# Cross-attention kernel: query weights on SyncE's queue, x in two parts around the first mask, one norm of twelve tiles behind eight maxima, and the shift placed ahead of two loads

## The chip, the cores and the metric

The kernel runs on one core of a Trainium2 chip. TensorE (PE in the rows, PEld for its weight loads), VectorE (DVE), ScalarE (ACT), GpSimd (POOL) and SyncE (SP) each work through their own instructions in order and meet at semaphores. DMAs are issued from the queues of SyncE (SPq) and ScalarE (ACTq). The metric is the time of one execution in device microseconds, as the median of several runs; a profiled execution gives the trace.

## The reference

Cross-attention with 16 heads of 8 over 32 batches, then a feed-forward block with quantised weights and activations. What is computed:

```
x   [32, 56, 128]   ctx [32, 1500, 128]   mask [32, 1, 56, 1500]
q = heads(layernorm(x) @ Wq + bq);  k = heads(ctx @ Wk + bk);  v = heads(ctx @ Wv + bv)
scores = where(mask == 0, -1e9, q k^T / sqrt(8))
x = x + (softmax(scores) v) @ Wo + bo
h = gelu(quant(layernorm(x)) @ ternary(w1)^T)
x = x + quant(h) @ ternary(w2)^T
```

## The kernel before

The work goes batch by batch, and every engine's order is written out by hand in tables of tokens (`PE_PASS`, `ACT_PASS`, `DVE_PASS`, `POOL_PASS`), one row of tokens per step. A step works on several batches at once: it takes the exponentials of batch b while it finds the maxima of batch b+1 and makes the keys of batch b+2. So two steps stand ahead of the first one that has all of it: `open` makes the keys of batch 0, and `lead` finds the maxima of batch 0 and makes the keys of batch 1. Then come `first_even`, `first_odd`, a loop of fourteen pairs of steps, two last steps and a tail.

The tokens that matter here. On TensorE: `T0` to `T2` turn a third of a batch's context (4 transposes each, L841), `K0` to `K2` make a third of the keys (L844), `V0` to `V2` of the values (L848), `X0` to `X3` turn four normalised tiles of x (L856), `Q0` to `Q7` project them (L858, two instructions of one `Q` to a row in a list of instructions), `F0` spreads a flag (L851), `M0` to `M11` are two matmuls each for the maxima (L902), `R0` turns the maxima (L853). On ScalarE `T`, `X` and `V` copy out of PSUM (L697, L702, L707), `sum` adds up a mask (L687), `kf` and `kh` make the keys and their rounded part (L717, L727). On VectorE `norm` normalises tiles of x (L1010 to L1043), `Q` takes a projection (L1143), `some` and `F0` make the flagged queries `q_flag` (L1120 to L1134), `bias` turns a mask into a bias (L1113), `m0` to `m23` take the maxima (L1206), two for each `M`. GpSimd makes the low part of the keys, `k_lo` (`kl`, L621 and L624), and the rounded and masked queries (`q`, L604 to L609), in the order `kl0 q0 kl1 kl2`.

PSUM has seven banks that go round in the order of TensorE's tokens; a token waits until what was in its bank has been taken. TensorE's `T0` of a step also waits until that batch's context has landed, and `M0`, `M4` and `M8` until a third of the keys has been placed.

SyncE places the keys (`place_keys`: for each third, wait for `k_lo`, two DMAs, wait for a copy, two more DMAs), places the shift (`place_shift`: wait for `shift_ready`, which VectorE sets after `R0`, then two DMAs that the first score matmul waits for, L930), and loads contexts and masks (`load`: 750 KB of context, then 656 KB of mask in two DMAs). It does these in one order, so each wait holds back all that stands behind it.

Of the kernel before, what the change touches and what calls it, by code (L numbers as in the profile page):

```python
# [205 lines left out]
def xattn_ffn(nc, x, ctx_in, mask, wq, bq, wk, bk, wv, bv, wo, bo, w1, w2, out):  # L206
    es = ExitStack()
    with es:
# [215 lines left out]
        def _(sp):  # L424
# [4 lines left out]

            def load(bt):  # L430
                b, k, p = bt
                at_ctx, at_mask = b * (SK * D), b * (SQ * SK)
                turned, biased = NSEG * (b - 1), NSEG * (b - 1)
                if not isinstance(b, int):
                    at_ctx, at_mask = sp.snap(at_ctx), sp.snap(at_mask)
                    turned = biased = sp.snap(turned)
                wait(sp, ctx_t_ready, turned)
                src = ctx_flat[bass.ds(at_ctx, SK * D)].rearrange("(c k d) -> k c d", k=KC, d=D)
                sp.dma_start(ctx_sb[:, p], src).then_inc(ctx_loaded[p], 16)
                wait(sp, mask_biased, biased)  # L440
                load_mask(at_mask, p)
# [222 lines left out]
        def _(act):  # L664

            ctx_0 = ctx_flat[0:SK * D].rearrange("(c k d) -> k c d", k=KC, d=D)
# [3 lines left out]
            act.dma_start(wk_sb[:], wk).then_inc(wk_loaded, 16)  # L670
            act.dma_start(bk_sb[:], bk.rearrange("(p a) -> p a", a=1)).then_inc(wk_loaded, 16)
            wq_groups = wq.rearrange("k (h g r) -> k g h r", h=2, g=2)
            bq_groups = bq.rearrange("(h g r a) -> h g r a", h=2, g=2, a=1)
            for g in range(2):
                for a in range(2):
                    act.dma_start(wq_sb[:, g, :].rearrange("k (h a r) -> k h a r", h=2, a=2)[:, :, a, :],
                                 wq_groups[:, g]).then_inc(wq_loaded, 16)
                    for h in range(2):
                        at = SLOT * h + GR * a
                        act.dma_start(bq_sb[at:at + GR, g:g + 1], bq_groups[h, g]).then_inc(wq_loaded, 16)  # L680
# [616 lines left out]
```

## Time and profile before

| | us |
|---|---|
| median of 3 runs | 914.86 |
| lowest and highest | 913.99, 914.88 |
| the profiled execution | 913.98 |
| its span in the trace | 912.3 |

The trace is of the profiled execution, so what is read from it is set against 913.98 us, of which 1.7 us lie outside the span; the median is 0.88 us above it. Times in the trace count from the start of the span. A row of the timeline gives the start, the time taken by the merged instructions, the engine, the line and operation, the tiles and shapes, the count, and in brackets how long the engine had been idle and what ended that. [...]

### The profile page before, as it was taken

How to read it: one execution, taken by the hardware profiler on the slowest of the kernel's cores; microseconds unless marked ns; L12 is line 12 of the kernel's file. 1: busy time of each engine (PE TensorE's matmuls, PEld its weight loads, DVE VectorE, ACT ScalarE, POOL GpSimd, SP SyncE). 2: the span in 40 equal slices, each digit the busy share in tenths (PEclk: the TensorE clock that was granted, in tenths of full speed). 3: DMA queues.
4: the chain of work that ended last, by engine and by line, in shares of the span. 5: the costliest groups of instructions: out<-in, count | busy, mean ns of one | idle time of the engine just before them, and what ended most of it. 6: DMA issues, size and time to landing. Idle time of an engine off the chain costs nothing.

```text
span 912.3 us, 33988 instructions
## 1 busy us (share of the span) xinstructions
PE 841.9 (92%) x11724; PEld 634.5 (70%) x11724; DVE 766.7 (84%) x2599; ACT 701.5 (77%) x1272; POOL 303.7 (33%) x360
## 2 busy tenths in 40 slices
PE   1676989999999999999999999999999999999993
PEld 1335767777777777777777777777777777777772
DVE  4887679888898989888898989888898989888954
ACT  1345768978797888979797888979797888979671
POOL 5512352323433333323433333322433333323300
PEclk9888999999999999999999999999999999999996
DMA  5433223343233333343233333343233323340100
GB/s 134 107 78 87 53 65 94 91 101 90 65 92 81 92 82 97 88 106 86 65 90 80 93 80 97 88 107 86 65 91 80 93 80 97 88 108 23 37 2 6
DMA packets 79000, 74.01 MB, mean 81 GB/s; under 512 B 10250, under 2 KB 75258, under 8 KB 78970
## 3 DMA queue, kind: packets, MB, share of 16 engines
q1 hardware_dynamic: 75695, 72.65, 31.0%
q10 hardware_dynamic: 3275, 0.97, 0.5%
q8 instruction: 18, 0.29, 0.1%
q14 instruction: 12, 0.10, 0.0%
HBM read 47.97 MB, written 0.92 MB: 54 GB/s over the span
## 4 chain that ended last, share of the span: by engine, by line
PE 64%; DVE 18%; issue 10%; ACT 3%; ACTq 2%; DMA 1%; DVEq 1%; SPq 1%; POOL 0%; POOLq 0%
PE ps_p L917 10%; PE ps_v L964 10%; PE ps_p L902 10%; PE ps_p L923 6%; PE ps_p L930 6%; PE ps_p L848 6%; PE ps_p L844 6%; DVE spare L1206 4%; PE ps_p L841 4%; DVE mask_bias L1113 1%; DVE row_stat L1025 1%; DVE row_stat L1026 1%; DVE row_stat L1024 1%; PE ps_p L872 1%; PE ps_p L868 1%
## 5 line engine op out<-in xcount | busy, mean ns | idle before, releaser
L1206 DVE CUSTOM_DVE_ANT_0 spare<-ps_p,mask_bias 120x500 bf16<-120x500 f32 x744 | 467.3, 673 | 49.0 <-PE ps_p L902 38.3
L737 ACT ACTIVATE probs<-ps_p 125x448 f32<-125x448 f32 x768 | 352.5, 559 | 57.1 <-PE ps_p L930 53.1
L621 POOL TENSOR_TENSOR k_lo<-k_full,keys 128x500 fp32r<-128x500 f32 x96 | 127.5, 1328 | 255.6 <-ACT keys L727 238.8
L917 PE MATMUL ps_p<-qry_lo,keys 64*125 64x448 f32 x768 | 162.8, 418 | 7.7 <-DVE seg_max L1206 2.6
L902 PE MATMUL ps_p<-keys,qry_hi 64*120 64x500 f32 x768 | 157.5, 430 | 5.6 <-DVE seg_max L1206 5.4
L964 PE MATMUL ps_v<-probs,vals 125*32 125x112 f32 x6144 | 160.7, 260 | 0.3 <-ACT probs L737 0.3
L964 PEld LDWEIGHTS ps_v<-probs,vals 125*32 125x32 f32 x6144 | 145.2, 110 | 22.4 <-issue 22.1
L923 PEld LDWEIGHTS ps_p<-qry_hi,keys 64*125 64x125 f32 x1536 | 146.0, 184 | 8.5
L930 PE MATMUL ps_p<-own_query,mask_bias 57*125 57x448 f32 x768 | 144.8, 370 | 7.5 <-DMA own_query<-shift 7.5
L923 PE MATMUL ps_p<-qry_hi,keys 64*125 64x224 f32 x1536 | 145.6, 266 | 0.0
L917 PEld LDWEIGHTS ps_p<-qry_lo,keys 64*125 64x125 f32 x768 | 72.5, 182 | 64.9 <-DVE seg_max L1206 33.0
L717 ACT ACTIVATE k_full<-ps_p,bk_sb 128x500 f32<-128x500 f32 x96 | 65.0, 677 | 65.7 <-PE ps_p L844 61.1
L604 POOL TENSOR_TENSOR q_hi<-q_flag,ones_f 128x112 fp32r<-128x112 f32 x32 | 13.7, 427 | 284.4 <-DVE q_flag L1134 284.4
L902 PEld LDWEIGHTS ps_p<-keys,qry_hi 64*120 64x120 f32 x768 | 69.2, 179 | 51.9 <-issue 20.8
L848 PE MATMUL ps_p<-wv_sb,ctx_t 128*125 128x128 f32 x768 | 102.8, 278 | 1.0 <-DVE seg_max L1206 1.0
L844 PE MATMUL ps_p<-ctx_t,wk_sb 128*128 128x500 f32 x192 | 101.8, 614 | 1.2 <-DVE seg_max L1206 1.1
L727 ACT ACTIVATE keys<-k_full 128x1000 fp32r<-128x1000 f32 x96 | 97.8, 1037 | 0.7
L848 PEld LDWEIGHTS ps_p<-wv_sb,ctx_t 128*125 128x125 f32 x768 | 92.0, 189 | 2.7 <-issue 1.6
L930 PEld LDWEIGHTS ps_p<-own_query,mask_bias 57*125 57x125 f32 x768 | 74.2, 186 | 8.0 <-DMA own_query<-shift 8.0
L697 ACT ACTIVATE ctx_t<-ps_p 128x500 f32<-128x500 f32 x96 | 55.0, 591 | 31.7 <-PE ps_p L841 31.7
L841 PE MATMUL ps_p<-ident,ctx_sb 125*128 125x125 f32 x384 | 59.0, 285 | 14.3 <-DMA ctx_sb<-in_ctx_dram 10.7
L841 PEld LDWEIGHTS ps_p<-ident,ctx_sb 125*128 125x128 f32 x384 | 46.7, 148 | 36.2 <-issue 20.1
(127 smaller groups left out, 885.1 us busy)
## 6 DMA issues: line engine op xcount, KB each, us to landing
keys<-k_lo SPq DMA_DIRECT2D x384, 62.5 KB, 2.0
ctx_sb<-in_ctx_dram SPq DMA_DIRECT2D x31, 750.0 KB
mask_sb<-in_mask_Bx1xSxS_ik_dram SPq DMA_DIRECT2D x64, 328.1 KB
own_query<-shift SPq DMA_DIRECT2D x64, 1.8 KB
out_dram<-x_rows SPq DMA_DIRECT2D x16, 56.0 KB, 1.6
ctx_sb<-in_ctx_dram ACTq DMA_DIRECT2D x3, 250.0 KB
x_rows<-in_x_dram SPq DMA_DIRECT2D x1, 672.0 KB, 12.7
w_sb<-in_L_ffn_w_dram SPq DMA_DIRECT2D x2, 256.0 KB, 7.2
```

The lines of the kernel that those rows point to most:

```text
L621: pool.tensor_tensor(k_lo[:, (p + n) % 2, :], k_full[:, (p + n) % 2, :], keys[:, p, 0, at].bitcast(F32), ALU.subtract)\
L727: act.activation(keys[:, p, 0:2, at], k_full[:, (p + n) % 2, :].rearrange("p (g k) -> p g k", g=1).to_broadcast([D, 2, SEG]), ACT.Copy).th ...
L737: act.activation(probs[:, (c + NG * p) % NP, h], ps_p[0:KC, BANK[how]["S", c, h], 0:HC], ACT.Exp)\
L841: mm = pe.transpose(bank[:, c * KC:(c + 1) * KC], ctx_sb[:, p, 4 * n + c, :], ident[0:KC, 0:KC])
L844: mm = pe.matmul(bank[:, 0:SEG], wk_sb[:], ctx_t[:, p, n * SEG:(n + 1) * SEG], start=True, stop=True)
L848: mm = pe.matmul(bank[0:KC, c * D:(c + 1) * D], ctx_t[:, p, at:at + KC], wv_sb[:], start=True, stop=True)
L902: pe.matmul(ps_p[0:MROWS, BANK[how]["M", n, h], 0:SEG], qry_hi[rows, p, 2 * r:2 * r + 2, :].rearrange("p a q -> p (a q)")[:, 0:MROWS], key ...
L917: pe.matmul(score_bank(c, h, how), keys[rows, p, 0, at], qry_lo[rows, p, :, :], start=True, stop=False, skip_group_check=True)
L923: pe.matmul(score_bank(c, h, how)[:, heads, :], keys[rows, p, 1 + g, at], qry_hi[rows, p, heads, 0:SQ], start=False, stop=False, skip_grou ...
L930: mm = pe.matmul(score_bank(c, h, how), mask_bias[rows, p, c * KC:(c + 1) * KC], own_query[rows, p, :, :], start=False, stop=True, skip_gr ...
L964: mm = pe.matmul(ps_v[r:r + VT, col:col + PAIR], with_ones(p, c, t), src, start=(c == 0 and t < 4), stop=(c == NC - 1), skip_group_check=True)
L1206: dve.tensor_tensor_reduce(junk, ps_p[0:MROWS, BANK[how][slot], 0:SEG], mask_bias[0:MROWS, p, s * SEG:(s + 1) * SEG].bitcast(F32), 1.0, LO ...
```

## The change

Six edits, all of them around the two steps ahead of the first full one.

- The query weights and biases go from ScalarE's queue (12 DMAs behind the context of batch 0) to SyncE's queue (8 DMAs, right behind the first four tiles of x). On ScalarE's queue the key weights now stand ahead of the context. ScalarE runs one small activation before its first wait.
- The other twelve tiles of x are sent when the first mask has landed, no longer right behind it.
- `norm` of these twelve tiles is one chain over all twelve, where there were three chains of four; it stands in `lead` behind `m7`. `X1` to `X3` and `Q2` to `Q7` all stand in `lead` behind it. The normalised tiles have a place of their own (in `probs`).
- On SyncE the keys of batch 0 are placed ahead of the load of batch 1's context and mask; they stood behind it.
- Batch 2's context is loaded ahead of batch 1's keys, and its mask behind the placing of the first shift, with `w1`, `w2` and the rows of `wo` behind that. They stood ahead of batch 1's keys.
- TensorE's wait for the rows of `wo` is at `W` in `first_odd`, no longer ahead of `first_even`.

```diff
 PE_PASS = passes(
-    "T0 X0 T1 T2 Q0 Q1 K0 F0 K1 K2 X1 Q2 Q3",
-    "M0 M1 T0 M2 T1 X2 M3 T2 Q4 Q5 M4 K0 M5 M6 K1 M7 X3 M8 K2 Q6 Q7 M9 V0 M10 F0 V1 M11 V2 R0",
+    "T0 X0 T1 T2 Q0 Q1 K0 K1 F0 K2",
+    "M0 M1 M2 T0 M3 T1 T2 K0 M4 K1 X1 Q2 Q3 M5 K2 M6 X2 Q4 Q5 V0 M7 X3 M8 Q6 Q7 V1 M9 F0 V2 M10 M11 R0",
...
 ACT_PASS = passes(
-    "T0 X0 T1 T2 sum kf0 kh0 kf1 kh1 kf2 kh2 X1",
-    "T0 T1 X2 T2 sum kf0 kh0 kf1 kh1 X3 kf2 kh2 V0 V1 V2",
+    "T0 X0 T1 T2 sum kf0 kh0 kf1 kh1 kf2 kh2",
+    "T0 T1 T2 sum kf0 kh0 kf1 kh1 X1 kf2 kh2 X2 V0 X3 V1 V2",
...
 DVE_PASS = passes(
-    "norm1 Q0 Q1 some F0 bias0 norm2 bias1 bias2 Q2 Q3",
-    "m0 m1 norm3 m2 m3 m4 m5 Q4 Q5 m6 m7 m8 m9 m10 m11 m12 m13 some m14 m15 Q6 Q7 "
-    + " ".join(f"m{n}" for n in range(16, 20)) + " F0 m20 m21 m22 m23 neg R0 bias0 bias1 bias2",
+    "Q0 Q1 some F0 bias0 bias1 bias2",
+    "m0 m1 m2 m3 m4 m5 m6 m7 norm1 m8 m9 Q2 Q3 m10 m11 m12 m13 Q4 Q5 some m14 m15 m16 m17 Q6 Q7 "
+    + " ".join(f"m{n}" for n in range(18, 20)) + " F0 m20 m21 m22 m23 neg R0 bias0 bias1 bias2",
...
             sp.wait_ge(mask_edge[0], 2)
             load_mask(0, 0)
+            sp.wait_ge(mask_loaded[0], 32)
             sp.dma_start(x_rows[:, 4:NT], x_groups[:, 4:NT]).then_inc(x_loaded[1], 16)
-            sp.wait_ge(ctx_loaded[0], 16)
-            sp.wait_ge(mask_edge[1], 2)
-            load(batch(0, 1))
-            sp.dma_start(wv_sb[:], wv).then_inc(wv_loaded, 16)
-            sp.dma_start(w1_sb[:], w1.rearrange("(a p) i -> p a i", p=128)).then_inc(ff_loaded, 16)
-            sp.dma_start(w2_sb[:], w2).then_inc(ff_loaded, 16)
-
             for n in range(NSEG):
                 place_keys(batch(0, 0), n)
+            load_context(batch(0, 1))
+            sp.wait_ge(mask_edge[1], 2)
+            load_mask_of(batch(0, 1))
+            sp.dma_start(wv_sb[:], wv).then_inc(wv_loaded, 16)
...
-            load(batch(0, 2))
+            load_context(batch(0, 2))
+            for n in range(NSEG):
+                place_keys(batch(0, 1), n)
+            place_shift(batch(0, 0))
+            load_mask_of(batch(0, 2))
+            sp.dma_start(w1_sb[:], w1.rearrange("(a p) i -> p a i", p=128)).then_inc(ff_loaded, 16)
+            sp.dma_start(w2_sb[:], w2).then_inc(ff_loaded, 16)
             sp.wait_ge(halves_known, 1)
...
-            for n in range(NSEG):
-                place_keys(batch(0, 1), n)
-            place_shift(batch(0, 0))
             step(batch(0, 0))
...
+            act.wait_ge(consts, 1)
+            act.activation(warm[:], ones_f[0:1, 0:1], ACT.Copy)
             act.wait_ge(wk_loaded, 32)
...
-                dve.wait_ge(x_loaded[min(g, 1)], 16)
-                if g > 1:
-                    dve.wait_ge(xn_copied, g - 1)
-                statistics(chain(group_step, 20 * g), x_rows[:, 4 * g:4 * g + 4, :], xn_stat[:], 4)
...
+                first, tiles = (0, 4) if g == 0 else (4, NT - 4)
+                dve.wait_ge(x_loaded[g], 16)
+                st = xn_stat[:, :, first:first + tiles]
+                statistics(chain(group_step, 20 * g), x_rows[:, first:first + tiles, :], st, tiles)
```

On SyncE's queue, from the first load to the placing of batch 1's keys, before (the first 1x8x56 row, `own_query`, is the shift; x_rows of 12 tiles are the rest of x):

```order
L506 DMA x_rows<-in_x_dram 112x4x128
L428 DMA mask_sb<-in_mask_Bx1xSxS_ik_dram 56x1500 x2
L509 DMA x_rows<-in_x_dram 112x12x128
L439 DMA ctx_sb<-in_ctx_dram 125x12x128
L428 DMA mask_sb<-in_mask_Bx1xSxS_ik_dram 56x1500 x2
L513 DMA wv_sb<-in_L_xattn_Wv_dram 128x128
L514 DMA w_sb<-in_L_ffn_w_dram 128x4x128
L515 DMA w_sb<-in_L_ffn_w_dram 128x512
L464 DMA keys<-k_lo 32x500 x12
```

And the same queue in the changed kernel, from the rest of x to the weights behind the shift:

```order
L529 DMA x_rows<-in_x_dram 112x12x128
L474 DMA keys<-k_lo 32x500 x12
L439 DMA ctx_sb<-in_ctx_dram 125x12x128
L430 DMA mask_sb<-in_mask_Bx1xSxS_ik_dram 56x1500 x2
L535 DMA wv_sb<-in_L_xattn_Wv_dram 128x128
L536 DMA wo_sb<-in_L_xattn_Wo_dram 128x128
L537 DMA bv_sb<-in_L_xattn_bv_dram 128x1
L538 DMA bo_sb<-in_L_xattn_bo_dram 112x128
L439 DMA ctx_sb<-in_ctx_dram 125x12x128
L474 DMA keys<-k_lo 32x500 x12
L459 DMA own_query<-shift 1x8x56 x2
L430 DMA mask_sb<-in_mask_Bx1xSxS_ik_dram 56x1500 x2
```

Batch 1's context, the fourth load of SyncE before, now stands behind the twelve DMAs that place batch 0's keys, and each third of those waits for GpSimd's `k_lo`.

On TensorE, from the projections of the first four tiles to the turning of batch 1's context, before (`qry_hi` and `keys` are the maxima's matmuls, `ident,ctx_sb` the turning of a third of a context, `ident,spare` that of four tiles of x):

```order
L858 MATMUL ps_p<-spare,wq_sb 128x448 x2
L844 MATMUL ps_p<-ctx_t,wk_sb 128x500
L851 MATMUL ps_p<-some_diag,ones_bf 128x56
L844 MATMUL ps_p<-ctx_t,wk_sb 128x500 x2
L856 MATMUL ps_p<-ident,spare 128x112 x4
L858 MATMUL ps_p<-spare,wq_sb 128x448 x2
L902 MATMUL ps_p<-keys,qry_hi 120x500 x4
L841 MATMUL ps_p<-ident,ctx_sb 128x125 x4
L902 MATMUL ps_p<-keys,qry_hi 120x500 x2
```

And from the same projections in the changed kernel, as far as the second four tiles of x:

```order
L872 MATMUL ps_p<-spare,wq_sb 128x448 x2
L858 MATMUL ps_p<-ctx_t,wk_sb 128x500 x2
L865 MATMUL ps_p<-some_diag,ones_bf 128x56
L858 MATMUL ps_p<-ctx_t,wk_sb 128x500
L916 MATMUL ps_p<-keys,qry_hi 120x500 x6
L855 MATMUL ps_p<-ident,ctx_sb 128x125 x4
L916 MATMUL ps_p<-keys,qry_hi 120x500 x2
L855 MATMUL ps_p<-ident,ctx_sb 128x125 x8
L858 MATMUL ps_p<-ctx_t,wk_sb 128x500
L916 MATMUL ps_p<-keys,qry_hi 120x500 x2
L858 MATMUL ps_p<-ctx_t,wk_sb 128x500
L870 MATMUL ps_p<-ident,probs 128x112 x4
```

`X1`, `Q2` and `Q3` have left the stretch ahead of the maxima; the turning of batch 1's context comes after `M2` where it came after `M1`, and `M3` to `M11` still stand behind it.

## Rows read from the trace of the kernel before

**Rows 1.** The page, part 1: busy time, share of the span and instructions:

```profile
PE 841.9 (92%) x11724; PEld 634.5 (70%) x11724; DVE 766.7 (84%) x2599; ACT 701.5 (77%) x1272; POOL 303.7 (33%) x360
```

**Rows 2.** Windows, a stretch of `lead`: busy us by engine, PEclk, DMA share, GB/s:

```profile
41.10:54.80 13.70, 8.51 (x26) 4.84 (x26) 10.21 (x42) 3.73 (x6) 2.89 (x6) 0.51 0.47 114
```

**Rows 3.** Timeline of TensorE in the opening and at the first score matmul:

```profile
13.40 1.04 PE L841 MATMUL ps_p<-ident,ctx_sb 125*128 125x125 f32 x4
18.29 1.10 PE L841 MATMUL ps_p<-ident,ctx_sb 125*128 125x125 f32 x4 [3.85 <-DMA ctx_sb<-in_ctx_dram]
24.01 3.33 PE L858 MATMUL ps_p<-spare,wq_sb 128*128 128x448 f32 x4 [4.63 <-DMA bq_sb<-in_L_xattn_bq_dram]
...
30.40 3.47 PE L844 MATMUL ps_p<-ctx_t,wk_sb 128*128 128x500 f32 x4
...
43.19 0.77 PE L902 MATMUL ps_p<-keys,qry_hi 64*120 64x500 f32 x2
...
78.78 0.74 PE L930 MATMUL ps_p<-own_query,mask_bias 57*125 57x448 f32 x2 [6.49 <-DMA own_query<-shift]
```

**Rows 4.** Timeline of VectorE, from the wait for the query biases to the flagged queries:

```profile
23.90 0.88 DVE L1010 BATCH_NORM_STATS2 xn_stat<-x_rows 112x6 f32<-112x128 f32 x4 [9.75 <-DMA bq_sb<-in_L_xattn_bq_dram]
...
42.55 0.67 DVE L1206 CUSTOM_DVE_ANT_0 probs<-ps_p,mask_bias 120x500 bf16<-120x500 f32 x1
...
43.74 0.87 DVE L1010 BATCH_NORM_STATS2 xn_stat<-x_rows 112x6 f32<-112x128 f32 x4
44.65 0.39 DVE L1014 BATCH_NORM_AGGREGATE xn_stat<-xn_stat 112x2 f32<-112x6 f32 x4
...
47.46 1.12 DVE L1043 TENSOR_SCALAR spare<-x_rows,xn_stat 112x128 f32<-112x128 f32 x4
48.49 0.67 DVE L1206 CUSTOM_DVE_ANT_0 probs<-ps_p,mask_bias 120x500 bf16<-120x500 f32 x1
...
53.16 0.68 DVE L1143 TENSOR_SCALAR q_all<-ps_p,bq_sb 128x448 f32<-128x448 f32 x1 [2.19 <-PE ps_p L858]
...
66.13 0.27 DVE L1134 TENSOR_TENSOR q_flag<-q_all,ps_p 128x112 f32<-128x112 f32 x1
```

**Rows 5.** Timeline of ScalarE: the table, the first keys, the sum of the weights:

```profile
19.62 1.28 ACT L697 ACT_TABLE_LOAD   x1 [19.62 <-issue]
...
28.21 0.68 ACT L717 ACTIVATE k_full<-ps_p,bk_sb 128x500 f32<-128x500 f32 x1 [3.91 <-PE ps_p L844]
...
86.04 0.63 ACT L742 ACTIVATE wtern<-w_sb 128x512 f32<-128x512 f32 x1
```

**Rows 6.** Timeline of GpSimd: the masked queries of batch 0:

```profile
33.05 1.15 POOL L607 TENSOR_TENSOR qry_hi<-head_of_row,q_hi 128x448 fp32r<-128x448 f32 x1
```

**Rows 7.** Timeline of SyncE's queue: what is issued, merged by kind:

```profile
4.20 0.78 SPq L428 DMA_DIRECT2D mask_sb<-in_mask_Bx1xSxS_ik_dram  x2
...
31.38 10.34 SPq L464 DMA_DIRECT2D keys<-k_lo  x12
...
76.24 1.47 SPq L449 DMA_DIRECT2D own_query<-shift  x2
77.75 0.46 SPq L439 DMA_DIRECT2D ctx_sb<-in_ctx_dram  x1
78.26 6.31 SPq L428 DMA_DIRECT2D mask_sb<-in_mask_Bx1xSxS_ik_dram  x2
91.81 2.46 SPq L464 DMA_DIRECT2D keys<-k_lo  x4
```

**Rows 8.** Windows while one context is loaded alone, columns as in rows 2:

```profile
77.70:79.00 1.30, 0.22 (x2) 0.22 (x4) 0.00 (x0) 0.00 (x0) 0.00 (x0) 0.50 0.02 5
79.00:81.00 2.00, 2.00 (x14) 1.83 (x16) 0.00 (x0) 1.25 (x3) 0.00 (x0) 0.50 0.27 82
81.00:84.50 3.50, 3.41 (x32) 2.59 (x30) 2.19 (x7) 3.10 (x8) 0.00 (x0) 0.88 0.36 109
84.50:87.00 2.50, 2.50 (x18) 1.33 (x16) 2.50 (x9) 2.28 (x7) 0.00 (x0) 1.00 0.88 212
```

More of the change, by code:

```diff
@@ L428, in load_mask, with load_context, load_mask_of @@
                     sp.dma_start(mask_sb[at:at + SQ, p, :], src).then_inc(mask_loaded[p], 16)
-            def load(bt):
[L431 to L441, printed above, removed]
+            def load_context(bt):
+                b, k, p = bt
+                at, turned = b * (SK * D), NSEG * (b - 1)
+                if not isinstance(b, int):
+                    at, turned = sp.snap(at), sp.snap(turned)
+                wait(sp, ctx_t_ready, turned)
+                src = ctx_flat[bass.ds(at, SK * D)].rearrange("(c k d) -> k c d", k=KC, d=D)
+                sp.dma_start(ctx_sb[:, p], src).then_inc(ctx_loaded[p], 16)
+            def load_mask_of(bt):
+                b, k, p = bt
+                at, biased = b * (SQ * SK), NSEG * (b - 1)
+                if not isinstance(b, int):
+                    at, biased = sp.snap(at), sp.snap(biased)
+                wait(sp, mask_biased, biased)
+                load_mask(at, p)
+            def load(bt):
+                load_context(bt)
+                load_mask_of(bt)
             def place_shift(bt):
@@ L506, in _ @@
             sp.dma_start(x_rows[:, 0:4], x_groups[:, 0:4]).then_inc(x_loaded[0], 16)
+            wq_groups = wq.rearrange("k (h g r) -> k g h r", h=2, g=2)
+            bq_groups = bq.rearrange("(h g r) -> h r g", h=2, g=2)
+            for a in range(2):
+                for g in range(2):
+                    sp.dma_start(wq_sb[:, g, :].rearrange("k (h a r) -> k h a r", h=2, a=2)[:, :, a, :],
+                                 wq_groups[:, g]).then_inc(wq_loaded, 16)
+                for h in range(2):
+                    at = SLOT * h + GR * a
+                    sp.dma_start(bq_sb[at:at + GR, :], bq_groups[h], allow_slow_non_contiguous=True).then_inc(wq_loaded, 16)
             sp.wait_ge(mask_edge[0], 2)
             load_mask(0, 0)
+            sp.wait_ge(mask_loaded[0], 32)
             sp.dma_start(x_rows[:, 4:NT], x_groups[:, 4:NT]).then_inc(x_loaded[1], 16)
-            sp.wait_ge(ctx_loaded[0], 16)
-            sp.wait_ge(mask_edge[1], 2)
-            load(batch(0, 1))
-            sp.dma_start(wv_sb[:], wv).then_inc(wv_loaded, 16)
-            sp.dma_start(w1_sb[:], w1.rearrange("(a p) i -> p a i", p=128)).then_inc(ff_loaded, 16)
-            sp.dma_start(w2_sb[:], w2).then_inc(ff_loaded, 16)
             for n in range(NSEG):
                 place_keys(batch(0, 0), n)
+            load_context(batch(0, 1))
+            sp.wait_ge(mask_edge[1], 2)
+            load_mask_of(batch(0, 1))
+            sp.dma_start(wv_sb[:], wv).then_inc(wv_loaded, 16)
             sp.dma_start(wo_sb[:], wo).then_inc(wo_loaded, 16)
@@ L540, in _ @@
             sp.wait_ge(stored, 16 * NT)
-        N_WQ = 12
+        N_WQ = 8
         N_WO = 3
@@ L664, in _ @@
         def _(act):
+            act.dma_start(wk_sb[:], wk).then_inc(wk_loaded, 16)
+            act.dma_start(bk_sb[:], bk.rearrange("(p a) -> p a", a=1)).then_inc(wk_loaded, 16)
             ctx_0 = ctx_flat[0:SK * D].rearrange("(c k d) -> k c d", k=KC, d=D)
@@ L669, in _ @@
                     .then_inc((ctx_loaded[0], ctx_second, ctx_third)[n], 16)
[L670 to L680, printed above, removed]
             def sum_mask(bt):
@@ L987, in _ @@
             step(batch(-1, 1), "lead")
-            pe.wait_ge(wo_rows_loaded, 16 * N_WO_ROWS)
             steps(pe, step)
@@ L1036, in norm_group @@
             def norm_group(g):
-                dve.wait_ge(x_loaded[min(g, 1)], 16)
-                if g > 1:
-                    dve.wait_ge(xn_copied, g - 1)
-                statistics(chain(group_step, 20 * g), x_rows[:, 4 * g:4 * g + 4, :], xn_stat[:], 4)
-                for r in range(4):
-                    ins = dve.tensor_scalar(xn[:, g % 2, r, :], x_rows[:, 4 * g + r, :], xn_stat[:, 6, r:r + 1],
-                                            xn_stat[:, 11, r:r + 1], ALU.subtract, ALU.mult)
-                ins.then_inc(xn_ready, 1)
+                first, tiles = (0, 4) if g == 0 else (4, NT - 4)
+                dve.wait_ge(x_loaded[g], 16)
+                st = xn_stat[:, :, first:first + tiles]
+                statistics(chain(group_step, 20 * g), x_rows[:, first:first + tiles, :], st, tiles)
+                for t in range(tiles):
+                    ins = dve.tensor_scalar(xn[:, first + t, :], x_rows[:, first + t, :], st[:, 6, t:t + 1],
+                                            st[:, 11, t:t + 1], ALU.subtract, ALU.mult)
+                    if t % 4 == 3:
+                        ins.then_inc(xn_ready, 1)
             def quantise_rows(st, part):
```

9 lines of the change are left out of this document (6 added, 3 removed).

## Prediction

> **What bounds the kernel now.** I read the page's busy shares first: TensorE is busy for 92% of the span, VectorE for 84% [rows 1]. Neither can lose anything in the loop, whose code the change doesn't touch; so the question is only when the full steps begin. The timeline gives that moment: the first score matmul (L930) at 78.78, when the shift has landed, after TensorE had been idle for 6.49 us [rows 3]. From there on the order of TensorE, VectorE, ScalarE and GpSimd is the old one (but for one wait, below), so I take what moves this moment to move the end by as much.
>
> What leads to it I followed back through the queues. The shift is issued at 76.24, behind the twelve DMAs for batch 1's keys [rows 7]; the last two thirds of those wait for GpSimd's `k_lo`, which in its order stands behind the masked queries, and these wait for VectorE's `q_flag` at 66.13 [rows 4]. From `q_flag` to the score it is 78.78 - 66.13 = 12.65 us. The order of GpSimd, and on SyncE of keys and shift, is the same in the changed kernel, so I keep these 12.65 us. **Everything hangs on when `q_flag` of batch 1 is made.** Ahead of it VectorE has 24 maxima, the norms and the projections, and in the opening it has one large hole: 9.75 us until the query biases land at 23.9 [rows 4].
>
> **The opening, up to the first maximum.** `T1` is done at 13.40 + 1.04 = 14.44 now; `T2` waits 3.85 us for the last third of batch 0's context [rows 3]. In the changed kernel neither the rest of x (672 KB) nor batch 1's context (750 KB) is in flight then, only 128 KB of query weights more on SyncE's queue. So I take `T2` to follow `T1`, and `Q0` to start at 14.44 + 1.10 = 15.5 where it starts at 24.01: 8.5 us earlier. The other end is that the third lands at 18.29 as now: 3.9 us less of a gain. The eight issues of weights and biases on SyncE put off the first mask (4.20 now [rows 7]) by some 5 us, an estimate from the 0.6 to 0.7 us of an issue there; at 109 to 212 GB/s [rows 8] its 656 KB have landed by 13 to 17. ScalarE sums it after `T2`'s copy at about 16: nothing for that, at most 1 us. Behind SyncE's new wait for this mask stand the rest of x and the key placements; these are due at 22.9 (below) and x, 672 KB, not until the norm at 46: nothing. The activation ahead of ScalarE's first wait brings the table load of 1.28 us forward from 19.62 [rows 5]; ScalarE is not due before `T0` and has time, so nothing.
>
> From `Q0` the chain is the old one: the first keys 28.21 - 24.01 = 4.2 us later [rows 3, 5], so at 19.7; the first placing DMA 31.38 - 28.21 = 3.17 us after that, at 22.9; the last of the twelve issued 10.34 us on [rows 7], at 33.2. A third of the keys takes 2.46 us to issue, and the shift takes 78.78 - 77.71 = 1.1 us from its issue to its reader [rows 3, 7]: `M0` at about 22.9 + 2.5 + 1.1 = 26.5. The masked queries, done at 33.05 + 1.15 = 34.2 now [rows 6], are done at 25.7, just before. With 0.77 us for the matmuls the first maximum comes at 27.3 instead of 42.55 [rows 3, 4]. That is 15 us, and the change would look like a large gain here.
>
> **What the gain runs into.** VectorE takes a maximum each 0.6 us (two from 42.55 to 43.74 [rows 4]). `m0` to `m5` are done at 27.3 + 3.6 = 30.9. `m6` needs `M3`, and on TensorE `M3` stands behind `T0`, which waits for batch 1's context. That load stands on SyncE behind the twelve key placements, so it is issued at 33.2. It used to be on its way before 10 us. Loaded alone, a context is issued at 77.75 [rows 7]; up to 79.0 almost nothing moves, then 2.0 us at 82 GB/s are 164 KB and 3.5 us at 109 GB/s 382 KB [rows 8]. Of 768 kB 222 are left at 84.5; there the queue moves 212 GB/s, but the mask behind it has a share, as it will have in the changed kernel. I put the end at 87.5, 9.8 us after the issue; bounds are 8.8 (all at 109 GB/s) and 11. So the context lands at 33.2 + 9.8 = 43.0.
>
> [...]
>
> `T0` (1.04) and `M3` (0.77) [rows 3] put `m6` at 43.0 + 1.8 = 44.8: **VectorE stands still from 30.9 to 44.8, 13.9 us.** The norm could fill this, since the rest of x has long landed, but it stands behind `m7`. So it starts at 46.0.
>
> **The norm of twelve.** A group of four takes 48.49 - 43.74 = 4.75 us: statistics 0.91, aggregates 0.39, twelve small steps 2.4, scaling 1.03 [rows 4]. Three times the first, second and last and once the small steps: 2.7 + 1.2 + 2.4 + 3.1 = 9.4 us against 3 x 4.75 = 14.25. This does save 4.9 us of VectorE. It ends at 55.4.
>
> **From there to `q_flag`.** Twelve maxima, six projections (0.65 each, near the 0.68 of [rows 4]) and 0.4 for `some`: 7.2 + 3.9 + 0.4 = 11.5 us. Before, the way from 48.49 to 66.13 is 17.64 us for 18 maxima and four projections, 10.8 + 2.6 + 0.4 = 13.8 of work and 3.8 of waits, 2.19 of them for one projection [rows 4]. In the changed kernel all of `X1` to `X3` and `Q2` to `Q7` lie in this stretch, each `Q` behind an `X` and ScalarE's copy, on a TensorE that has stood still during the norm; I take 5 us of waits. `q_flag` is at 55.4 + 16.5 = 71.9, 5.8 us later than now.
>
> **The loads behind the shift.** Batch 2's mask, `w1`, `w2` and the rows of `wo` are issued after the shift, about 1 us before the first score. ScalarE reads `w1` 86.04 - 78.78 = 7.3 us after it [rows 3, 5]; 656 + 512 KB at 109 to 212 GB/s [rows 8] take 5.6 to 11 us after the 1.3 us of start. I take nothing, and 2 us as the other end, because ScalarE would be late and TensorE runs on for some banks. SyncE then gets to batch 2's keys later; it is free from 78.26 + 6.31 = 84.57 until 91.81 now [rows 7], and about 6 us of issues move in. Nothing, at most 1 us. Moving TensorE's wait for the rows of `wo` costs nothing, since it comes a step later.
>
> **Sum.** The profiled execution took 913.98 us; 913.98 + 5.8 = 919.8, and the median lies 0.9 us above the profiled one: I say 920. In short `q_flag` = landing of batch 1's context + 1.8 + 1.2 + 9.4 + 16.5, that is landing + 28.9, and it breaks even where the context lands at 37.2.
>
> **Rivals.**
> [...]
> - *The context comes at the queue's higher rate.* At 212 GB/s [rows 8] it takes 1.3 + 3.6 = 4.9 us and lands at 38.1: +0.9 us, 914.9, no change. Against it: 3.5 us at 109 GB/s with nothing else in the queue. [...]
> - *Faster: the load is early enough.* Place: SyncE's key placements. Of the 10.34 us only some 12 x 0.62 = 7.4 are issue, the rest waits for GpSimd, which in the changed kernel has VectorE's company less. If these waits go, the load is issued 3 us sooner, at 30.2, and at 212 GB/s lands at 35.1: `q_flag` at 64.0, 2.1 us early, 911.9. It decides from a landing before 37.2. With no wait at all the formula's end is 32.1 + 9.4 + 16.5 = 58.0, 8 us early, 906. Against it: both must go well.
>
> **How the numbers follow.** Forecast 0.62, with 916.5 to 923.5 as its own range (landing 8.8 to 11 us after the issue, waits of 3 to 7 us, `T2` late, up to 2 us behind the shift). TensorE slow: 0.15. No change: 0.11. Faster: 0.12. What a measurement of this kernel can tell from no change is about 0.2%, 1.8 us. The slower side is the forecast and the slow TensorE, 0.77. The range runs from 913, which leaves out the faster case, to 927, which takes in a slow TensorE with a late `T2`.
>
> **What would show it.** In the profile of the changed kernel: `Q0` near 15.5; the first maximum near 27; then a hole of over 10 us on VectorE that ends with `m6`, with TensorE's `T0` waiting for the context; a chain of twelve after that, some 9.4 us long; `q_flag` of batch 1 near 72 and the first score 12.65 us later, near 84.6. The prediction is wrong if the hole is under 6 us, if the context lands within 5 us of its issue, or if the time from the first score to the end is not what it was (913.98 - 78.78).

## The result, and the profile after

The changed kernel takes 925.76 us (median of four runs, 924.39 to 929.03) where the kernel before takes 914.87 beside it: ratio 1.0126, interval 1.0105 to 1.0146. It is slower, as forecast and inside the range (913 to 927), but by 10.9 us and not by 5.1. The profiled execution took 924.39 us, its span is 922.3.

VectorE of the changed kernel, timeline (start, time, idle time before and what ended it), the rows that answer to [rows 4]; L1221 are the maxima, L1023 to L1057 the norm:

```profile
28.98 0.68 DVE L1221 CUSTOM_DVE_ANT_0 probs<-ps_p,mask_bias 120x500 bf16<-120x500 f32 x1 [6.06 <-issue]
...
47.84 0.68 DVE L1221 CUSTOM_DVE_ANT_0 probs<-ps_p,mask_bias 120x500 bf16<-120x500 f32 x1 [15.18 <-PE ps_p L916]
...
49.12 2.42 DVE L1023 BATCH_NORM_STATS2 xn_stat<-x_rows 112x6 f32<-112x128 f32 x12
...
53.38 1.24 DVE L1044 SCALAR_TENSOR_TENSOR xn_stat<-xn_stat 112x12 f32<-112x12 f32 x1
54.65 0.50 DVE L1046 SCALAR_TENSOR_TENSOR xn_stat<-xn_stat 112x12 f32<-112x12 f32 x1
55.19 0.17 DVE L1043 TENSOR_TENSOR xn_stat<-xn_stat 112x12 f32<-112x12 f32 x1
...
59.49 0.68 DVE L1221 CUSTOM_DVE_ANT_0 probs<-ps_p,mask_bias 120x500 bf16<-120x500 f32 x1
...
75.43 0.27 DVE L1149 TENSOR_TENSOR q_flag<-q_all,ps_p 128x112 f32<-128x112 f32 x1
```

The first maximum is 13.6 us earlier than before, and then VectorE stands for 15.18 us ahead of `m6`. What it waits for is seen on TensorE and SyncE, timelines of the same kernel (answering to [rows 3, 7]):

```profile
16.40 1.09 PE L855 MATMUL ps_p<-ident,ctx_sb 125*128 125x125 f32 x4 [2.39 <-DMA ctx_sb<-in_ctx_dram]
17.29 2.63 PE L872 MATMUL ps_p<-spare,wq_sb 128*128 128x448 f32 x4
...
45.86 1.10 PE L855 MATMUL ps_p<-ident,ctx_sb 125*128 125x125 f32 x4 [16.19 <-DMA ctx_sb<-in_ctx_dram]
```

```profile
24.05 10.10 SPq L474 DMA_DIRECT2D keys<-k_lo  x12
...
34.19 0.48 SPq L439 DMA_DIRECT2D ctx_sb<-in_ctx_dram  x1
```

`T0` waits for the context, which SyncE issues only behind the twelve key placements, and which lands 45.86 - 34.19 = 11.67 us later. The windows of that stretch and of the one around the first score at 88.03 (busy us of PE, PEld, DVE, ACT, POOL, then TensorE's granted clock, whose records in every trace here hold only 1.00 and 0.50, the half clock of the text, then DMA share, GB/s):

```profile
35.00:41.00 6.00, 0.00 (x0) 0.00 (x0) 0.00 (x0) 0.00 (x0) 0.80 (x2) 0.50 0.32 92
41.00:45.80 4.80, 0.00 (x0) 0.00 (x0) 0.00 (x0) 0.00 (x0) 0.00 (x0) 0.50 0.90 186
...
88.00:94.30 6.30, 6.27 (x40) 5.63 (x42) 2.29 (x7) 3.92 (x8) 0.00 (x0) 0.50 0.85 205
94.30:97.00 2.70, 2.69 (x20) 1.51 (x18) 2.54 (x9) 2.69 (x7) 0.00 (x0) 1.00 0.34 95
```

The sum of the profiled execution, 924.39 - 913.98 = 10.41 us, is `q_flag` at 75.43 instead of 66.13, +9.30; from it to the first score 12.60 instead of 12.65, -0.05; and from the first score to the end 836.36 instead of 835.20, +1.16.

### The profile page after: what moved, and what is told of

Its sections match the earlier page's. It is cut to its first block, busy times and chain, and to the rows that moved or that the text cites. A ratio compares the mean times of both kernels' runs of the same rounds, so it can differ in the third digit from the quotient of the medians.

```text
span 922.3 us, 33972 instructions
## 1 busy us (share of the span) xinstructions
PE 840.9 (91%) x11724; PEld 635.3 (69%) x11724; DVE 760.7 (82%) x2575; ACT 702.0 (76%) x1273; POOL 303.6 (33%) x360
## 4 chain that ended last, share of the span: by engine, by line
PE 66%; DVE 17%; issue 8%; DMA 3%; ACT 2%; SPq 1%; POOL 1%; DVEq 1%; ACTq 0%; POOLq 0%
PE ps_v L978 11%; PE ps_p L916 10%; PE ps_p L931 10%; PE ps_p L937 7%; PE ps_p L944 7%; PE ps_p L862 6%; PE ps_p L858 6%; DVE spare L1221 4%; PE ps_p L855 4%; DMA ctx_sb<-in_ctx_dram 3%; DVE mask_bias L1128 1%; DVE row_stat L1039 1%; DVE row_stat L1037 1%; DVE row_stat L1038 1%; PE ps_p L886 1%
## 5 line engine op out<-in xcount | busy, mean ns | idle before, releaser
L1221 DVE CUSTOM_DVE_ANT_0 spare<-ps_p,mask_bias 120x500 bf16<-120x500 f32 x744 | 467.6, 674 | 49.5 <-PE ps_p L916 37.9
L624 POOL TENSOR_TENSOR q_hi<-q_flag,ones_f 128x112 fp32r<-128x112 f32 x32 | 13.6, 426 | 299.4 <-DVE q_flag L1149 299.4
```

The costliest lines, as they stand in the source:

```text
L1221: dve.tensor_tensor_reduce(junk, ps_p[0:MROWS, BANK[how][slot], 0:SEG], mask_bias[0:MROWS, p, s * SEG:(s + 1) * SEG].bitcast(F32), 1.0, LO ...
```

## The experiments

**1. The place of the load.** My theory: the load's place behind the keys makes the loss. Against it: the new orders of the engines, a slow TensorE, or contention that would come with an early load. The changed kernel with one line moved:

```diff
+            load_context(batch(0, 1))
             for n in range(NSEG):
                 place_keys(batch(0, 0), n)
-            load_context(batch(0, 1))
```

> The changed kernel with one line moved: batch 1's context load is issued ahead of the twelve placements of batch 0's keys instead of behind them. Theory (the place of this load on SyncE makes the whole loss): issued at about 14.5 it lands before 30, T0 follows M2 without a wait, the hole of 15.18 us ahead of m6 on VectorE goes, m7 ends near 34.2, the norm of twelve near 44.6 and, with the same 15.9 us of tail, q_flag is made near 60.5 instead of 75.43. With 12.6 us to the first score and 836.4 from there the execution takes about 909.5 us (907 to 912), below the kernel before. Rival 1 (the load at the head of the queue slows the keys or the rest of x): m0 later than 31, 912 to 915. Rival 2 (TensorE at half clock binds next, so the tail grows to 20 us): 913 to 916. Rival 3 (the place of the load is not the cause): 924.

Measured: 913.24 us, ratio to the kernel before 0.998 (0.997 to 0.9989). The whole loss is gone, but the gain that the theory added to it (907 to 912 us) came only in part. The first score is at 75.96, 12.07 us earlier than in the changed kernel, `q_flag` at 62.41. TensorE and ScalarE, timelines:

```profile
28.68 1.60 PE L916 MATMUL ps_p<-keys,qry_hi 64*120 64x500 f32 x6 [5.54 <-DMA keys<-k_lo]
30.21 1.09 PE L855 MATMUL ps_p<-ident,ctx_sb 125*128 125x125 f32 x4
...
45.71 3.36 PE L872 MATMUL ps_p<-spare,wq_sb 128*128 128x448 f32 x4 [3.24 <-ACT spare L713]
```

```profile
40.41 1.45 ACT L698 ACTIVATE mask_sum_junk<-mask_sb 56x1500 bf16<-56x1500 int32 x1 [5.92 <-DMA mask_sb<-in_mask_Bx1xSxS_ik_dram]
...
45.13 0.53 ACT L713 ACTIVATE spare<-ps_p 128x448 f32<-128x448 f32 x1
```

`T0` no longer waits. The 1.9 us by which `q_flag` is later than expected have a new wait: ScalarE sums batch 1's mask, which still stands behind the keys, and the copy of `X1` stands behind this sum (3.24 us). So the tail from the norm's end to `q_flag` grew from 15.94 to 19.05 us. The time is that of the second rival, but the clock isn't the reason: the same two projections at half clock took 3.36 us here and 3.35 in the changed kernel. From `q_flag` to the first score it was 13.55 us instead of 12.60. The rest of the missing gain lies behind the first score: 837.70 us from there to the end.

**2. The same fault in the kernel before.** Batch 1's context load alone is put behind the keys, everything else as it was:

```diff
...
-            load(batch(0, 1))
+            load(batch(0, 1), "m")
...
             for n in range(NSEG):
                 place_keys(batch(0, 0), n)
+            load(batch(0, 1), "c")
```

> The kernel before with one part of the change alone: batch 1's context load stands behind the twelve placements of batch 0's keys; all else, orders of the engines too, as before. Theory (the place of this load costs wherever it is put behind the keys): issued near 41.7 it lands 9.8 to 11.7 us later, near 52.5, m2 near 54 instead of 48.5; so 5.8 us later, less 0 to 3 us which the opening gains when this load no longer shares its queues with the third part of batch 0's context and the query biases: 918 us (915 to 921). Rival (the loss comes from the new orders of the engines, not from the load): 911 to 915.

Measured: 921.67 us, ratio 1.0075 (1.0058 to 1.0091), 0.7 us above the theory's range. TensorE of this kernel, timeline:

```profile
53.27 1.09 PE L844 MATMUL ps_p<-ident,ctx_sb 125*128 125x125 f32 x4 [12.81 <-DMA ctx_sb<-in_ctx_dram]
```

Issued at 43.45, landed 9.82 us later, `q_flag` at 70.92 (+4.79). The old orders lose 6.9 us by the same move, where the new ones lose 12.5 (925.76 against 913.24); in the old ones a norm of four stands in the hole (44.54 to 49.29). The expected gain in the opening did not come: `T2` was at 21.46, later than the 18.29 of [rows 3]; batch 1's mask now stood further up in the queue, but that this is the reason was not tried.

**3. Work in the hole.** The late load stays; the norm of twelve goes ahead of `m6`:

```diff
-    "m0 m1 m2 m3 m4 m5 m6 m7 norm1 m8 m9 Q2 Q3 m10 m11 m12 m13 Q4 Q5 some m14 m15 m16 m17 Q6 Q7 "
+    "m0 m1 m2 m3 m4 m5 norm1 m6 m7 m8 m9 Q2 Q3 m10 m11 m12 m13 Q4 Q5 some m14 m15 m16 m17 Q6 Q7 "
```

> The changed kernel with the norm of twelve ahead of m6 instead of behind m7 in VectorE's order; the late context load stays. VectorE then norms in the hole, from 32.6 to about 43. Theory A (VectorE's work alone sets q_flag): m6 at 47.8 as before, m7 to 49.1, tail 15.9: q_flag near 65.0, 914 us. Theory B (TensorE's chain behind the late context takes over): from T0 at 45.86 to K1's end at 52.09 nothing changes, X1 starts there instead of at 57.59, and the way from X1 to F0 keeps its 16.6 us: q_flag near 70, 919 us (917 to 921). If the norm's place didn't matter: 924.

Measured: 919.84 us (ratio 1.0053), `q_flag` at 70.46: theory B. The norm ran from 33.46 to 42.52, yet half of its 10 us came back as waits of VectorE for TensorE, whose own chain behind the late context takes from 46.84 to about 70. So the prediction's formula, landing + 28.9, would not have held for other orders: a second chain lies only 5 us under VectorE's.

**4. How long a context takes.** The place stays late; the load is cut in two:

```diff
...
-            load_context(batch(0, 1))
+            src_1 = ctx_flat[SK * D:2 * SK * D].rearrange("(c k d) -> k c d", k=KC, d=D)
+            sp.dma_start(ctx_sb[0:112, 1], src_1[0:112]).then_inc(ctx_loaded[1], 16)
+            sp.dma_start(ctx_sb[112:KC, 1], src_1[112:KC]).then_inc(ctx_rest, 16)
...
```

> The changed kernel, with batch 1's context loaded by two DMAs, partitions 0 to 111 and 112 to 124, instead of one over 125 partitions; place in the queue unchanged. Theory (the load takes 11.7 us because its 125 partitions are spread over few DMA engines, as its share of 0.31 to 0.36 and 106 to 109 GB/s say; 112 partitions can use all 16): it is issued at 34.2, moves at 200 GB/s or more and has landed near 39.5, T0 starts 6.4 us earlier than 45.86, q_flag near 69, 918 us (916.5 to 919.5). Rival (the rate is set by the memory, the bytes per packet or the queue): landing and time unchanged, 924.

Measured: 920.16 us (ratio 1.0054), 0.7 us above the theory's range, since the context landed at 41.5 and not at 39.5. TensorE's `T0` in the timeline, and a window of the load:

```profile
41.52 1.06 PE L860 MATMUL ps_p<-ident,ctx_sb 125*128 125x125 f32 x4 [11.08 <-DMA ctx_sb<-in_ctx_dram]
```

```profile
36.00:40.00 4.00, 0.00 (x0) 0.00 (x0) 0.00 (x0) 0.00 (x0) 0.59 (x2) 0.50 1.00 224
```

Issued at 34.98 and landed 6.54 us later instead of 11.67; the DMA share is 1.00 where it was 0.32, at 224 GB/s instead of 92 (a part of the 224 is already the mask behind the context). So the place in the queue and the memory don't hold the rate at 92 GB/s. Nor is it that there are two DMAs: in the changed kernel the rest of x, one DMA of 672 KB over 112 partitions, lands 4.8 us after its issue. What differs is the number of partitions: in the traces the semaphore of the load over 125 rises in 5 steps as its data lands (45.48 to 45.82 in the changed kernel), that of the load over 112 in 16 (39.55 to 40.87), and that of the 13 behind it in 13 (39.91 to 41.38). An estimate from the windows agrees with the steps: a share of 0.32 of the 16 engines is 5.1 of them, and 1.00 is all 16. How the number of partitions leads to the number of engines, no run shows.

**5. The time behind the first score.** The loads behind the shift are put back ahead of batch 1's keys and of the shift:

```diff
             load_context(batch(0, 2))
-            for n in range(NSEG):
-                place_keys(batch(0, 1), n)
-            place_shift(batch(0, 0))
             load_mask_of(batch(0, 2))
...
+            for n in range(NSEG):
+                place_keys(batch(0, 1), n)
+            place_shift(batch(0, 0))
             step(batch(0, 0))
```

> The changed kernel with batch 2's mask, w1, w2 and the rows of wo back ahead of the placements of batch 1's keys and of the shift, as in the kernel before. The question is where the time behind the first score went: 836.36 us there in the changed kernel, 835.20 before. Theory A (TensorE's granted clock sets it): over the first stretches behind the first score TensorE was granted half the clock for 6.4 us before, 9.7 in the changed kernel, 12.2 to 12.6 with the context ahead or in two DMAs, and the time from the first score to the end was 835.2, 836.4, 837.5 to 837.7, so 835.2 + 0.4 x (half-clock time - 6.4); that rule holds here too, whatever half-clock time comes out (835.2 to 838). Theory B (the loads behind the shift hold the first step up): the time from the first score to the end falls back to 835.2 even where the half-clock time stays at 9.7 or more, and the execution takes 923.2 us. By both the first score stays within 1 us of 88.0.

Measured: 926.30 us (ratio 1.0113); first score at 89.78, 0.8 us beyond what both theories allowed; in the profiled run of 927.64 us there are 837.86 us behind it. Theory B falls: without these loads in flight (DMA share 0.31 instead of 0.85) the time behind the first score didn't fall back, it was 1.5 us longer. Windows of this kernel, and then of the kernel before, around the first score:

```profile
89.80:95.60 5.80, 5.80 (x38) 5.22 (x40) 1.85 (x5) 3.92 (x8) 0.00 (x0) 0.50 0.31 89
95.60:98.00 2.40, 2.36 (x20) 1.48 (x16) 2.40 (x9) 2.06 (x5) 0.00 (x0) 0.99 0.83 191
```

```profile
78.80:81.80 3.00, 3.00 (x20) 2.77 (x22) 0.00 (x0) 1.96 (x4) 0.00 (x0) 0.50 0.28 85
81.80:84.00 2.20, 2.13 (x24) 1.59 (x20) 1.69 (x5) 1.89 (x5) 0.00 (x0) 1.00 0.36 109
```

TensorE comes out of its wait for the shift at half clock each time, but is granted the full one 3.0 us after the first score in the kernel before, 6.3 in the changed one, 5.8 here; 47.8 to 51.2 us behind that a second stretch at half clock, 3.4 or 6.8 us long, follows in every kernel. The table has both together, from the clock records of each profiled execution up to 200 us:

| kernel | half clock from the first score on, us | first score to end, us |
|---|---|---|
| before | 6.5 | 835.2 |
| experiment 8 (norm first) | 6.5 | 836.5 |
| experiment 6 (x without the wait) | 9.6 | 836.4 |
| the changed kernel | 9.7 | 836.4 |
| 3 (norm in the hole) | 9.7 | 836.5 |
| 2 (before, context behind) | 10.9 | 836.7 |
| 10 (norm 4 and 8) | 11.8 | 837.5 |
| 4 (context 112 + 13) | 12.2 | 837.5 |
| 7 (context and mask ahead) | 12.3 | 837.6 |
| 9 (contexts in two) | 12.4 | 838.1 |
| 1 (context ahead) | 12.7 | 837.7 |
| 5 (loads ahead) | 12.7 | 837.9 |

The time behind the first score goes with the half clock in all but experiment 8, which is 1.3 us over the rule that I had set down. Where the time is lost can be read from VectorE: its maxima behind the first score are the same in every kernel, so the start of one, counted from the first score, can be set against the same one before. How much later it comes than in the kernel before, in us:

| the maximum that starts before at | 88.50 | 129.81 | 148.27 | 870.31 (the last) |
|---|---|---|---|---|
| the changed kernel | 0.79 | 0.81 | 0.55 | 0.91 |
| experiment 1 | 0.64 | 0.66 | 1.85 | 2.24 |
| experiment 5 | 0.67 | 0.69 | 1.89 | 2.41 |
| experiment 8 | 0.02 | 0.02 | 0.05 | 0.52 |

The loss comes in the two stretches at half clock and not between them. Behind them 0.4 to 0.5 us more gather over the rest of every kernel, experiment 8 included, and another 0.4 lie outside the span (2.1 us there, 1.7 before); for these no run shows a reason. So experiment 8 had no loss in the half-clock stretches, as the rule says, and its 1.3 us came later. The four runs of the changed kernel show the same: 924.39 and 924.92 us at a mean granted clock of 0.969, 926.60 at 0.966, 929.03 at 0.963. That the clock is the cause of the loss up to 148 us is read from this agreement, and from the loads being ruled out; no run held the clock up by itself.

**6. SyncE's wait for the first mask.** It is taken out, and x is sent at once:

```diff
-            sp.wait_ge(mask_loaded[0], 32)
```

> The changed kernel without SyncE's wait for the first mask, so that the rest of x (672 KB) is sent at about 7.4 instead of 13.99. Theory (in the opening the third part of batch 0's context, the mask and x share the transfer rate, and the wait is what brought T2 from 18.29 to 16.40): T2 goes back to 17.5 to 18.5, the mask lands later, too, so ScalarE's sum may hold the first keys, and all up to the context load comes 1 to 3 us later: 925.5 to 927.5. Rival (the wait does nothing, T2's part is slow by itself): T2 at 16.4 and 924.4.

Measured: 928.41 us (ratio 1.0153): `T2` at 19.81 instead of 16.40, behind a wait of 5.78 us for its third of the context, and the first score is 3.60 us later than in the changed kernel. The theory holds, with a size above its range (925.5 to 927.5): this wait of SyncE's is worth some 3 us to the changed kernel. The prediction used it (x is not in flight while the third lands) and looked only for what it might cost.

**7. Context and mask ahead.** As in experiment 1, with batch 1's mask moved, too:

```diff
-            for n in range(NSEG):
-                place_keys(batch(0, 0), n)
             load_context(batch(0, 1))
             sp.wait_ge(mask_edge[1], 2)
             load_mask_of(batch(0, 1))
+            for n in range(NSEG):
+                place_keys(batch(0, 0), n)
```

> The changed kernel with batch 1's context and mask both ahead of the placements of batch 0's keys. With the context alone moved ScalarE stood 5.92 us before its sum of batch 1's mask (issued at 34.8, behind the keys), the copy of X1 behind it came 3.2 us late and q_flag at 62.41. Theory (the mask was the next wait): the sum no longer waits, Q2 starts some 3 us earlier, q_flag near 59.2, first score near 72.5, and with 835.2 to 837.7 behind it 908 to 911 us. Rivals: the mask's second DMA holds SyncE past 24 and the keys come late (912 to 915); the wait is replaced by another one at the same place (913).

Measured: 912.57 us, ratio 0.9972 (0.9963 to 0.9982); `q_flag` at 61.93. ScalarE's wait is gone (TensorE waits 0.63 us for the copy of `X1`) and the tail is 3.6 us shorter than in experiment 1, but most of this was lost ahead of it: `m0` came 1.84 us later, and the norm took 10.3 us instead of 9.0. The time is that of the first rival. SyncE's queue, timeline:

```profile
14.36 8.93 SPq L430 DMA_DIRECT2D mask_sb<-in_mask_Bx1xSxS_ik_dram  x2
25.39 10.10 SPq L474 DMA_DIRECT2D keys<-k_lo  x12
```

Issuing the mask's two DMAs, 0.84 us elsewhere in this queue, held SyncE for 8.93 us with the slow context load ahead of them. But that hold was over at 23.29, and from there SyncE stood until 25.39 for GpSimd's `k_lo`, so it isn't what made the keys late, as the rival had it. Of the 1.84 us `k_lo` makes 0.74; the other 1.1 lie between the first placing DMA and `M0` (5.12 us instead of 4.03), where the DMA share was 0.52 instead of 0.38. That the mask in flight slowed the placing is read from this share; no run tried it.

**8. The norm ahead of m0.** As 7, with

```diff
-    "m0 m1 m2 m3 m4 m5 m6 m7 norm1 m8 m9 Q2 Q3 m10 m11 m12 m13 Q4 Q5 some m14 m15 m16 m17 Q6 Q7 "
+    "norm1 m0 m1 m2 m3 m4 m5 m6 m7 m8 m9 Q2 Q3 m10 m11 m12 m13 Q4 Q5 some m14 m15 m16 m17 Q6 Q7 "
```

> As the run with context and mask ahead, and the norm of twelve ahead of m0, into the 6.06 us in which VectorE waits for the first keys. Theory (VectorE's and TensorE's orders then have no hole): the norm runs from 23 to 33.5, m0 to m7 end at 38.5, X1 follows K1 at about 36, the way from X1 to F0 takes 16.6 us, q_flag near 53.5, first score near 66.5, 902 to 905 us. Rival (VectorE's norm and GpSimd's work on the keys slow each other, as before from 33.07 to 38.55, where small steps took 0.5 to 1.17 us instead of 0.17): the norm takes 13 to 14 us and the keys come 3 us later; q_flag near 57, 906 to 909.

Measured: 912.74 us (ratio 0.9976), `q_flag` at 62.12: no gain over 7, and outside what both had put. The norm took 13.0 us (23.15 to 36.09) where in experiment 1 it took 9.0, and since `M3` waits for a bank that a maximum must free (3.17 us, until 37.41), TensorE's `T1`, `T2` and the keys came late with it. The rival was right about the norm, and its price too low.

**9 and 10. Without the slow load, and with a norm that fits.** As 7, with both opening contexts (three DMAs on ScalarE's queue, one on SyncE's) cut at partition 112:

```diff
...
-                act.dma_start(ctx_sb[:, 0, 4 * n:4 * n + 4], ctx_0[:, 4 * n:4 * n + 4])\
-                    .then_inc((ctx_loaded[0], ctx_second, ctx_third)[n], 16)
+                for lo, hi, done in ((0, 112, (ctx_loaded[0], ctx_second, ctx_third)),
+                                     (112, KC, (ctx_rest[0], ctx_second, ctx_third))):
+                    act.dma_start(ctx_sb[lo:hi, 0, 4 * n:4 * n + 4], ctx_0[lo:hi, 4 * n:4 * n + 4])\
+                        .then_inc(done[n], 16)
...
```

> As the run with context and mask ahead of the keys, and both opening contexts (the three parts of batch 0's on ScalarE's queue, batch 1's on SyncE's) loaded by two DMAs each, partitions 0 to 111 and 112 to 124. With the mask ahead SyncE stood 8.93 us in issuing it, until 23.3, and the first key placement came at 25.39 instead of 24.05; T2 came at 16.27. Theory (the 125-partition loads use few DMA engines and what is behind them waits): T2 near 14.5, the mask's issue under 5 us, the first key placement near 22, q_flag near 59, first score near 71.5, 907 to 910 us. Rival (in the opening the whole rate of the queues is used up already, so the parts only change places): T2 at 16 or later, 911 to 914 us.

And then also the norm of twelve in two:

```diff
-                first, tiles = (0, 4) if g == 0 else (4, NT - 4)
+                first, tiles = ((0, 4), (4, 4), (8, NT - 8))[g]
...
-    "m0 m1 m2 m3 m4 m5 m6 m7 norm1 m8 m9 Q2 Q3 m10 m11 m12 m13 Q4 Q5 some m14 m15 m16 m17 Q6 Q7 "
+    "norm1 m0 m1 m2 m3 m4 m5 m6 m7 norm2 m8 m9 Q2 Q3 m10 m11 m12 m13 Q4 Q5 some m14 m15 m16 m17 Q6 Q7 "
```

> As the run with both contexts in two DMAs, and the norm of twelve taken in two: four tiles ahead of m0, in the 6 to 7 us in which VectorE waits for the first keys, eight behind m7. Theory (a short norm fits the gap even at the slow steps of VectorE beside GpSimd, and X1 no longer waits for the whole norm): m0 at most 1 us later, X1 behind K1 at about 35, the norm of eight from 35 to 42, X2 near 41, then some 10 us to F0 and ten maxima and six projections of work: q_flag near 54, first score near 66.5, 902 to 906 us. Rival (ScalarE's copy of X1 or TensorE's half clock set the way instead): q_flag near 58, 906 to 909. If the norm's place gives nothing, as with all twelve ahead of m0: the time of the run without it.

Measured, for 9 and 10: 908.80 us, ratio 0.9935 (0.9912 to 0.9958), and 907.33 us, ratio 0.9916 (0.9899 to 0.9932): both are faster than both kernels; between the two the difference is not clear of the noise. In experiment 9 `T2` follows `T1` without a wait, the mask's issue takes 0.81 us, and the first key placement comes at 20.77. TensorE of experiment 9, timeline:

```profile
12.97 1.87 PE L864 MATMUL ps_p<-ident,ctx_sb 125*128 125x125 f32 x8
14.63 2.01 PE L881 MATMUL ps_p<-spare,wq_sb 128*128 128x448 f32 x4
```

So the theory for 9 holds (907 to 910). In experiment 10 `q_flag` is at 56.91, only 0.71 us ahead of 9, and not at 54; the time is that of its rival (906 to 909). Its norm of four took 9.4 us beside GpSimd (below), `M3` waited 2.68 us for a bank, and the first projections 1.88 us for ScalarE's copy of `X1`.

## Why the prediction was right, and where it was wrong

Right was the mechanism, step by step: the first maximum at 28.98 (forecast 27.3), the context issued at 34.19 (33.2), `T0` waiting for it, a hole of 15.18 us (13.9) that ends with `m6`, the norm behind `m7`, `q_flag` to first score 12.60 (12.65). Experiment 1 takes the cause away and 2 puts it into the kernel before.

Wrong were sizes. The forecast of 920 was 5.8 us short. Of these 0.7 are a slip in the sum: 919.8 for the profiled execution and 0.9 for the median make 920.7. `q_flag` at 75.43 instead of 71.9 makes 3.5, the time behind the first score 1.2, and the medians 0.5. The terms:

- *`T2` to follow `T1`.* It came at 16.40, 2.0 us later than put, and half of this reached the issue of the load, 1.0 us late. The third of the context was slow through its 125 partitions: experiment 9 cuts it (and batch 1's context, issued only at 12.74) and has `Q0` at 14.63. Batch 1's context isn't the reason, since with it in flight `T2` came at 16.46 and 16.27 (experiments 1 and 7); x would have been one (experiment 6).
- *Landing 9.8 us after the issue, at most 11.* It was 11.67, outside my bounds: +1.9 us, the largest miss, and the step that failed. I had put the end of the sample of [rows 8] at 87.5 from its bytes. In the trace of the kernel before the sample's last bytes did move at 87.75, but the semaphore that TensorE waits for had its last step at 88.86, 11.1 us after the issue. So 1.3 us of the miss stood in the trace before: 0.25 in the bytes, and 1.1 from the last bytes to the semaphore, which I had put at nothing. The changed kernel added some 0.5: up to 41.0 its load went as the sample (0.32, 92 GB/s), then mask, wv, wo and batch 2's context shared the queue with its last part. In experiment 2, where no mask follows at once, the load took 9.82 us; that this is the forecast number is chance, since the sample had the mask behind it.
- *The norm of twelve, 9.4 us.* It was 10.37: +1.0 us. Alone it takes 9.0 (experiments 1 and 3); the rest is two small steps of 1.24 and 0.50 us, while GpSimd made the low part of a key.
- *The tail of 16.5 us* was 15.94, with 4.2 us of waits instead of 5: -0.6. In it TensorE had half the clock until 63.6 and the full one from there on. The chance of 0.15 and the end of the range at 927 rest on a TensorE at half clock throughout `lead`, which would make 924; no run shows such a `lead`. In the changed kernel the clock was 0.50 from 26.0 to 49.9 and from 56.8 to 63.6, and 1.00 between them and from there to 84.1.
- *Nothing behind the first score.* It was 1.16 us, one of my own signs of being wrong, and I had named loads as its only possible cause. Experiment 5 rules them out. About half of it, 0.55 us, goes with TensorE's clock, which I had weighed for `lead` and not for the first full steps; the rest gathers later and outside the span, and its cause stays open. The medians add 0.5 us: the changed kernel's is 1.4 us above its profiled run, that of before 0.9.

What is left, some 0.3 us, lies in the way from the landing to the norm (3.26 us, put at 3.0).

The rivals with a faster or unchanged kernel needed the context by 37 to 38. In experiment 4 not even the load with a DMA share of 1.00 got there from that place: it landed at 41.5. Of all the kernels here, those with the load ahead of the keys are at or below the time before, and those with it behind them all above it.

## What to carry to other kernels

When a step is moved to the front of a queue, list what its move leaves behind it, and follow each of these to its reader in the other engines' orders: here a gain of 13.6 us at the first maximum was lost to one load of 750 KB. A load is priced by its own rate from a stretch of the trace where the same load runs, up to the step of the semaphore and not only to the last byte; and that rate may be its shape's and not the memory's (92 GB/s over 125 partitions, 224 GB/s over 112 and 13 with the mask behind them). Cutting it at 112 partitions was worth 5.6 us behind the keys, and cutting both opening contexts 3.8 us with the loads ahead of them. A time saved ahead of a waiting TensorE need not be passed on in full: behind the wait it ran at half clock for 3.0 us in the kernel before and for 6.3 us in the changed one.

## What the runs showed of the hardware

- *Small steps of VectorE beside GpSimd.* VectorE and GpSimd of experiment 10, timelines of the same stretch:

```profile
25.42 1.10 DVE L1052 TENSOR_TENSOR xn_stat<-xn_stat 112x4 f32<-112x4 f32 x1
...
27.10 1.17 DVE L1055 SCALAR_TENSOR_TENSOR xn_stat<-xn_stat 112x4 f32<-112x4 f32 x1
```

```profile
25.25 1.25 POOL L646 TENSOR_TENSOR k_lo<-k_full,keys 128x500 fp32r<-128x500 f32 x1
...
27.01 1.24 POOL L646 TENSOR_TENSOR k_lo<-k_full,keys 128x500 fp32r<-128x500 f32 x1
```

  Here steps of 0.16 us last until GpSimd's instruction is over (26.52 and 26.50, 28.27 and 28.25); in the changed kernel the 1.24 us at 53.38 end with GpSimd's of 53.34. Statistics of 2.41 us that began at 23.15 in experiment 8, beside a GpSimd instruction of 23.01, were not slowed. In the kernel before, six of the eight small steps between 33.07 and 39.06 took 0.51 to 1.17 us beside GpSimd, and from 45.08 on, with GpSimd idle, each took 0.16 or 0.17. Which instructions of the two engines hold each other, and why, the runs don't show.
- *The issuer is held by the next DMA behind a slow load.* Two mask DMAs took 8.93 us to issue right behind a context load over 125 partitions (experiment 7), 0.99 behind the keys (experiment 1), and 0.81 behind the context in two DMAs, whose second took 2.40 (experiment 9). It is not the mask: in experiment 2 the 64 KB of wo, right behind such a load, took 5.94 us to issue.
- *From the last byte to the semaphore.* In the kernel before, the context of [rows 8] had moved at 87.75, and its semaphore was complete at 88.86, 1.1 us later.
- *TensorE's clock after a wait.* After 4.9 to 6.5 us of standing ahead of the first score, it was granted 0.50 of the clock for 3.0 us (before) to 6.3 us (the changed kernel) of matmuls almost without a break, in every kernel here.
